# A third buffer for one-hot rows and weighed planes, with the second chunk's rows and the first deltas on GpSimd

## The reference

```
def step(h, inp):
    dt_t, B_t, C_t, u_t = inp
    dA = jnp.exp(dt_t[..., None] * A)
    h = dA * h + (dt_t * u_t)[..., None] * B_t[:, None, :]
    return (h, jnp.einsum('bdn,bn->bd', h, C_t))
```

```
in_blk = (br == bc) & (br < num_blocks)
attn_mask = attn_mask.at[b_safe, rl, cl].set(1.0)
edge_feats = edge_feats.at[b_safe, rl, cl].set(ef_flat)
```

## Time and profile before

| | |
|---|---|
| median of three runs | 597.03 us |
| the profiled execution, its own time | 597.8 us |
| its span in the profile | 596.1 us |
| DVE busy | 469.8 us (79%) |
| PE busy (modelled ends) | 424.2 us (71%) |
| POOL busy | 342.8 us (58%) |
| ACT busy | 199.3 us (33%) |
| POOL L929, 64 steps | 152.5 us |
| DVE L1577, 64 scans | 146.2 us |
| DVE L662, 3 weighed planes | 6.9 us |
| DVE L1506, 48 one-hot rows, mean of one 279 ns | 9.6 us of durations that overlap |

### The profile page before, as it was taken

The page is one execution under the profiler, slowest core; times in us unless marked ns, Lnnn a source line. Parts: engine busy times, 40 slices in busy tenths (PEclk is TensorE's granted clock), DMA queues, the critical chain, the costliest instruction groups (busy, mean ns, idle before and its releaser), DMA issues.

```text
span 596.1 us, 8784 instructions
## 1 busy us (share of the span) xinstructions
PE 424.2 (71%) x3287; PEld 208.3 (35%) x3288; DVE 469.8 (79%) x580; ACT 199.3 (33%) x228; POOL 342.8 (58%) x304
## 2 busy tenths in 40 slices
PE   6785864757667667766767788999644797556495
PEld 2462313323222222222222334467542444543131
DVE  1999998899999999999999634799987555996021
ACT  2656785313223322332232044230102107212132
POOL 5766102749999998999899733189973000051100
PEclk8968897569999999999999989875557798557776
DMA  8650023845564556455544000000000000000000
GB/s 286 190 143 9 3 71 91 185 99 143 143 172 137 147 152 168 141 142 156 160 143 106 1 3 12 1 2 2 3 4 21 0 1 1 1 2 2 11 8 36
DMA packets 29819, 46.15 MB, mean 77 GB/s; under 512 B 18440, under 2 KB 19884, under 8 KB 28748
## 3 DMA queue, kind: packets, MB, share of 16 engines
q1 hardware_dynamic: 27340, 45.15, 27.6%
...
...
## 4 chain that ended last, share of the span: by engine, by line
DVE 32%; POOL 29%; PE 21%; issue 12%; ACT 2%; DMA 2%; ACTq 0%; DVEq 0%; POOLq 0%; SPq 0%
POOL dBu L929 14%; POOL hit L913 6%; PE ps L2080 4%; POOL work L1010 3%; DVE hC L1598 3%; PE ps L2408 2%; DVE hC L1368 2%; PE ps L2584 2%; POOL work L1015 2%; DVE hst L1577 2%; DVE hC L1364 2%; POOL work L999 2%; PE ps L2288 2%; PE ps L2605 1%; DVE work L1866 1%
## 5 line engine op out<-in xcount | busy, mean ns | idle before, releaser
L2218 PE MATMUL ps<-hC,ident 128*128 128x512 f32 x256 | 122.8, 602 | 0.0
L1208 ACT ACTIVATE ps<-work,a_neg 128x1020 f32<-128x1020 f32 x64 | 71.2, 1115 | 152.4 <-DVE hst L1577 102.6
L1577 DVE TENSOR_TENSOR_SCAN hst<-ps,dBu 128x1024 f32<-128x1024 f32 x43 | 98.2, 2284 | 5.0 <-POOL dBu L929 3.8
L2202 PE MATMUL ps<-late,pick_state 96*128 96x512 bf16 x128 | 40.4, 399 | 68.9 <-DVE hC L1598 67.6
L913 POOL DMA_INDIRECT hit<-in_L_attn_edge_values,tab_i x64 | 64.6, 1010 | 27.6 <-DMA hit<-in_L_attn_edge_values,tab_i 18.0
L929 POOL TENSOR_TENSOR dBu<-work,dA 128x1024 f32<-128x1024 f32 x32 | 75.3, 2359 | 6.6 <-DMA dA<-b_rows_all 3.8
L2218 PEld LDWEIGHTS ps<-hC,ident 128*128 128x128 f32 x256 | 49.7, 194 | 43.6 <-issue 35.2
L929 POOL TENSOR_TENSOR dBu<-work,b_sb 128x1024 f32<-128x1024 f32 x16 | 39.5, 2471 | 38.7 <-DVE dA L1506 37.2
L1598 DVE TENSOR_TENSOR hC<-hst,ps 128x1024 f32<-128x1024 f32 x43 | 51.4, 1195 | 1.8 <-PE ps L2202 1.8
L2202 PEld LDWEIGHTS ps<-late,pick_state 96*128 96x128 bf16 x128 | 7.9, 98 | 120.6 <-DVE hC L1598 116.9
L1577 DVE TENSOR_TENSOR_SCAN work<-ps,dBu 128x1024 f32<-128x1024 f32 x21 | 48.0, 2284 | 1.5 <-POOL dBu L929 0.8
...
## 6 DMA issues: line engine op xcount, KB each, us to landing
...
hit<-in_L_attn_edge_values,tab_i POOLq DMA_INDIRECT x64, 3.8
...
```

The costliest lines, as they stand in the source:

```text
L1208: nc.scalar.activation(dst[:, :, 1:], src[:, :, 1:], ACT.Exp, scale=a_neg[:, n:n + 1]).then_inc(dA_sb, 1)
L1577: V.tensor_tensor_scan(h_buf[i % 3], dA_ps[k], dBu[:, k, :], 0.0, ALU.mult, ALU.add).then_inc(scan_done, 1)
L2202: last = T.matmul(bank(2 + h), pick_state[:, n, :, :].rearrange("p v i -> p (v i)"), parts[:, j * NT + h * HALF:j * NT + (h + 1) * HALF], ...
L2218: last = T.matmul(bank(6 + h), ident[:, :], hC[:, i % 2, h * HALF:(h + 1) * HALF], start=False, stop=(n == S - 1))
```

## The change

Chunk 2 gets buffers of its own: rows in the unused part of `late`, planes in `sq`. So DVE no longer waits for `hot_used` 1 before chunk 2, SP's loads into `dA` wait for `hot_used` 1 in place of `planes_ps`, and scan(1) no longer waits for `planes_ps`. POOL now makes the 16 rows of chunk 1 (`second_rows`) and the first group's two deltas (`first_delta`), ahead of its step 0, whose wait for `rows_sb` 3 is gone. PE waits for POOL's rows (`rows_pool`) ahead of chunk 1. Late in the kernel, the wait for `s2_merged` between two DVE instructions becomes the chain's own wait at the same place.

```diff
-        row_hot = [halves(t[:, :, :]).rearrange("p (s r) -> p s r", r=N) for t in (dA, dBu)]
+        row_hot = [halves(t[:, :, :]).rearrange("p (s r) -> p s r", r=N) for t in (dA, dBu)] + \
+            [late[:, 2 * NT:4 * NT].bitcast(BF16).rearrange("p (s r) -> p s r", r=N)]
-        plane_hot = [hst[:, k, :].bitcast(BF16).rearrange("p (s k c) -> p s k c", k=PLANES, c=C)
-                     for k in range(2)]
+        plane_hot = [t.bitcast(BF16).rearrange("p (s k c) -> p s k c", k=PLANES, c=C)
+                     for t in (hst[:, 0, :], hst[:, 1, :], sq[:, :])]
...
                 if i == 2:
-                    sp.wait_ge(planes_ps, 1)
+                    sp.wait_ge(hot_used, 1)
...
                     pool.wait_ge(hot_used, 2)
-                    pool.wait_ge(rows_sb, SLOTS // CHUNK)
...
+            def second_rows():
+                pool.wait_ge(cols_sb, 1)
+                for s_ in range(CHUNK):
+                    last = nc.gpsimd.tensor_scalar(row_hot[1][:, s_, :], rows_at[:, :],
+                                                   d_at[:, CHUNK + s_:CHUNK + s_ + 1], None, ALU.is_equal)
+                last.then_inc(rows_pool, 1)
+            def first_delta():
+                pool.wait_ge(dt_log, 1)
+                nc.gpsimd.tensor_tensor(dt_act[:, 0:NT], dt_act[:, 0:NT], dtu[:, 0:NT], ALU.add).then_inc(dt_sb, 1)
+                pool.wait_ge(dt_sb, 1)
+                nc.gpsimd.tensor_tensor(dtu[:, 0:NT], dt_act[:, 0:NT], u_act[:, 0:NT], ALU.mult).then_inc(dtu_sb, 1)
+            second_rows()
+            first_delta()
             state_input(0)
...
-            for q in range(SLOTS // CHUNK):
-                if q >= 2:
-                    dve.wait_ge(hot_used, q - 1)
-                if q < 2:
-                    weigh_planes(V, q % 2, q)
-                    hot_rows(q % 2, q).then_inc(rows_sb, 1)
-                else:
-                    dve.wait_ge(dt_log, 1)
...
-                    hot_rows(q % 2, q).then_inc(rows_sb, 1)
-                    weigh_planes(V, q % 2, q).then_inc(rows_sb, 1)
+            weigh_planes(V, 0, 0)
+            hot_rows(0, 0).then_inc(rows_sb, 1)
+            weigh_planes(V, 1, 1).then_inc(rows_sb, 1)
+            dve.wait_ge(dt_parts, J)
+            dve.wait_ge(b_rows_sb, 1)
+            V.memset(dA_ps[0][:, 0:NT:N], 0.0)
+            V.memset(dA_ps[1][:, 0:NT:N], 0.0).then_inc(dA_zero, 1)
+            hot_rows(2, 2).then_inc(rows_sb, 1)
+            weigh_planes(V, 2, 2).then_inc(rows_sb, 1)
...
-                if i == 1:
-                    dve.wait_ge(planes_ps, 1)
...
-                V.copy_predicated(scores2[:, :, 1, :], older.bitcast(I32).unsqueeze(1).to_broadcast([P, SEGS, C]),
-                                  scores2[:, :, 0, :]).then_inc(s2_merged, 1)
+                link(V.copy_predicated(scores2[:, :, 1, :], older.bitcast(I32).unsqueeze(1).to_broadcast([P, SEGS, C]),
+                                       scores2[:, :, 0, :]))
...
-                dve.wait_ge(s2_merged, u + 1)
...
                 pe.wait_ge(rows_sb, q + 2 if ends else q + 1)
-                put_chunk(q % 2, ends).then_inc(planes_ps if ends else hot_used, 1)
+                if q == 1:
+                    pe.wait_ge(rows_pool, 1)
+                put_chunk(q, ends).then_inc(planes_ps if ends else hot_used, 1)
```

More of the change, by code:

```diff
@@ L367, in hybrid_kernel @@
         rows_sb = sem("rows_sb")
+        rows_pool = sem("rows_pool")
         hot_used = sem("hot_used")
@@ L413, in hybrid_kernel @@
         v2_ps = sem("v2_ps")
-        s2_merged = sem("s2_merged")
         v2_sb = sem("v2_sb")
@@ L1549, in _ @@
             dve.wait_ge(cols_sb, 1)
-            for q in range(SLOTS // CHUNK):
-                if q >= 2:
-                    dve.wait_ge(hot_used, q - 1)
-                if q < 2:
-                    weigh_planes(V, q % 2, q)
-                    hot_rows(q % 2, q).then_inc(rows_sb, 1)
-                else:
-                    dve.wait_ge(dt_log, 1)
-                    V.tensor_tensor(dt_act[:, 0:NT], dt_act[:, 0:NT], dtu[:, 0:NT], ALU.add).then_inc(dt_sb, 1)
-                    dve.wait_ge(dt_sb, 1)
-                    V.tensor_tensor(dtu[:, 0:NT], dt_act[:, 0:NT], u_act[:, 0:NT], ALU.mult).then_inc(dtu_sb, 1)
-                    dve.wait_ge(dt_parts, J)
-                    dve.wait_ge(b_rows_sb, 1)
-                    V.memset(dA_ps[0][:, 0:NT:N], 0.0)
-                    V.memset(dA_ps[1][:, 0:NT:N], 0.0).then_inc(dA_zero, 1)
-                    hot_rows(q % 2, q).then_inc(rows_sb, 1)
-                    weigh_planes(V, q % 2, q).then_inc(rows_sb, 1)
+            weigh_planes(V, 0, 0)
[7 more added lines that the diff above has]
+            weigh_planes(V, 2, 2).then_inc(rows_sb, 1)
             def state_scan(i):
```

## The result

The changed kernel takes 601.18 us (median of eight runs, 599.83 to 603.28) against 597.5 us for the kernel before, measured beside it (594.74 to 600.82, also eight). The ratio is 1.0071, 95% interval 1.0048 to 1.0095: slower, by 3.7 us of the medians.

The account below looks back on a forecast made before the run. No engine was taken as the bound throughout; what counts is when the state loop gets into step, at the scan behind the edge table. +14.9 us at scan(2) less 1.35 at the table gave +13.6, 610.6 us, range 602 to 616.

Parts of the forecast that it names:

- step 1: Behind planes 0, DVE's chunk 0 rows alternate with POOL's rows: 16 turns of 0.94 us, 15.0 us, both ending at 101.1.
- Steps 2 to 4: POOL's deltas end at 103.4 and 107.9, PE's chunk 1 at 107.6, dBu(0) at 110.3, DVE's planes 2 at 117.6.
- Step 5: PE's chunk 2 ends at 121.25 in place of 106.05, +15.2 us; hC(0) is 15.2 later, scan(2) 14.9.
- Step 6: At the edge table, only dBu(4) lies across L1523 and L1524: 1.75 us in place of 3.1, -1.35 us.
- The bf16 rows don't exclude POOL: Faster rival: DVE's rows keep 0.196 us beside POOL's, which end at 97.7; 592.8 us, chance 0.11.
- DVE's run goes first: Rival: DVE's queued rows keep the port, POOL's other 15 rows end at 110.5; +8.7 us, 605.7 us, chance 0.21.
- Nothing measurable: Rival: POOL's row is cheap and loses few turns, or a dearer row eats the gain; 595 to 599 us, chance 0.05.
- The faster sign: The outcome that the changed kernel is faster than before, given 0.11; same had 0.05, slower 0.84.

Follow-up runs that it names:

- tt6: Probe: the kernel before with the third buffer and deltas behind planes 2 on DVE, plus six unused two-operand POOL additions of 256 f32 columns; 597.67 us, one run.
- delta_only: Changed kernel with chunk 1's rows back on DVE, so POOL makes only the first deltas ahead of its step 0; 595.68 us, ratio 0.9977 to before.
- ts12: Probe: the kernel before with the third buffer and deltas behind planes 2 on DVE, plus 12 unused one-hot POOL rows of 256 bf16 columns; 594.53 us, one run.
- psum_planes: Changed kernel with the planes' weights first copied into PSUM and the two PSUM clears moved behind planes 2; 594.12 us, ratio 0.9955 to before.
- ts_wide: Probe: the kernel before with third buffer and deltas behind planes 2 on DVE, plus three unused POOL multiplications of 512 f32 columns by a scalar; 593.88 us, one run.

## Why the prediction had the sign and missed the size

**The step that failed** is step 1 of the forecast, "turn by turn": 16 turns of 0.94 us, in which each DVE row waits for a whole POOL row, so that chunk 0's rows end at 101.1. They ended at 90.36. The price of the POOL row was right (0.86 taken, 0.90 measured alone); the exclusion was not: DVE's rows took 0.26 us each on average, not 0.94. The rows that it was taken from the earlier trace rows show DVE's `tensor_scalar` stuck behind dBu, which has two operands. The changed kernel's POOL row has one. With two operands on POOL the turns are there, row for row (tt6, and the 2.20 us of delta_only); with one, four DVE rows pass in each POOL row and lose 0.22 us together (ts12). The prediction's text had named its own test, "DVE's rows stay at 0.196 beside POOL's", and that is nearly what happened.

That the sign came out all the same was luck. The forecast had DVE held up by POOL; in the runs POOL was held up by DVE's planes (6.5 us, and 6.40 us of the stretch in psum_planes). Without that hold the kernel is faster than before.

The sentence on the Trainium skill, SBUF — State Buffer, "Who interferes with whom", falls with it for this pair. That a `tensor_scalar` in a two-port mode and GpSimd block each other for the whole instruction is not what ts12 shows, with four rows in each POOL row of 1.02 us; here the measurement decides. tt6 agrees with the sentence. No trace shows in which mode DVE's rows ran.

**Steps 2 to 4.** The first delta ended at 108.01 in place of 103.4, the second at 110.43 (107.9), and dBu(0) at 112.85 (110.3): 2.5 to 4.6 us later than forecast. POOL's rows ended at 105.70 in place of 101.1, because planes 1 and 2 stopped them for 4.3 us. Step 1 had only planes 0 in it (POOL's rows start at 86.1 there), for by its turns DVE came to planes 1 when POOL's rows were done; as DVE's rows passed, planes 1 started at 90.28 and planes 2 at 96.43, in the midst of them. That a plane stops POOL was in the earlier trace rows (dBu(0) at 4.17 us beside planes 2). On DVE all was far earlier: planes 2 ended at 98.70, not 117.6. So the one failed step moved both ends, and against each other: DVE's was 19 us too late in the sum, POOL's dBu(0) 2.5 us too early.

**Step 5.** Chunk 2 was to end on PE at 121.25 (+15.2); it ended at 112.44 (+6.4). hC(0) moved by 117.46 - 111.65 = 5.8 us, scan(2) by 5.5 (14.9 forecast). What hC(0) waits for is no longer the planes, whose last copy ends at 115.90, but scan(1), and behind it POOL's dBu.

**Step 6.** The mechanism was right in the main, and the term half as large: L1540 waited for dBu(4) alone, as forecast, and the two operations that were to take 1.75 us took 2.51 (121.90 to 124.41) against 3.11 before, -0.60 in place of -1.35. The forecast had dBu(4) end 1.25 us after the table's start; it ended at 123.90, 2.00 us after it, because it was not released by scan(2)'s end (120.86) but stood behind dBu(3), which ended at 121.59. The sum of the steps as measured is +5.46 at scan(2) and -0.60 at the table, +4.86; the scan behind it moved by 4.85.

**The rivals.** *The bf16 rows don't exclude POOL* was right about DVE's rows, and wrong about the time, for it let POOL's rows run to 97.7 as if the planes weren't there; they ran to 105.70. With the planes out of POOL's way the time is 594.12 us, near its 592.8. *DVE's run goes first* did not happen: POOL's rows went on at 1.0 us each beside DVE's. *Nothing measurable*: the interval excludes no change, and its lower end (1.0048) lies at the bound of 0.5%. The faster sign, which the rivals gave 0.11, was one copy away (psum_planes).

**What stays open**: why a one-operand POOL operation takes 0.22 us from DVE's rows with 256 bf16 columns and 0.64 with 512 columns of f32. Columns, bytes and operation changed together in ts_wide. Nor do these probes tell whether it is the second operand itself that makes an addition hold every row.
